# Attention, a gated FFN in FP4 and their residuals on one core: a new attention opening, presets of the residual in PSUM and another drain

## The chip, the core and the metric

One core of one Trainium2 chip. The time is the device time of one execution in microseconds. The engines are TensorE (PE in the rows, its weight loads PEld), VectorE (DVE), ScalarE (ACT), GpSimd (POOL) and SyncE (SP), which issues all DMAs here. Each runs its own instructions in order; they wait for each other by semaphores only.

## The reference, cut to what matters

x is [64, 128, 256] fp32, the context has the same shape.

```python
def attn(Q, K, V, Wq, bq, Wout, bout):          # auto-correlation attention, one head of 16 columns
    q, k, v = (Q @ Wq + bq).T, (K @ Wq + bq).T, (V @ Wq + bq).T
    corr = real(ifft(fft(q) * conj(fft(k)))).mean(axis=(0, 1))      # 128 lags
    W, I = top_k(corr, 12); W = softmax(W)
    R = sum(w * roll(v, -shift) for w, shift in zip(W, I))
    return reshape(broadcast(R, 16 heads), [B, L, 256]) @ Wout + bout
def fp4_linear(x, w):                            # both sides quantised in blocks of 16 to the E2M1 grid
    return quant(x) @ quant(w).T
x = x + attn(layernorm(x), ctx, ctx, ...)
n = layernorm(x)
x = x + fp4_linear(silu(fp4_linear(n, w_gate)) * fp4_linear(n, w_up), w_down)      # 256 -> 704 -> 256
```

## The kernel before, in words

A tile is one of the 64 sequences, 128 rows by 256 columns; two tiles make a pair, so there are NP = 32 pairs. All of x stays in SBUF (`xs`).

First phase (to about 70 us): x and the context are loaded, turned by TensorE, projected and correlated; beside it the weights are quantised. Then comes the opening of the second phase: the correlation's sum (L855), the twelve largest lags on VectorE (L1091 to L1109), two DMAs that turn the weights of the lags into the circulant matrix `cT` (L359, L361), `wp` (L867 and L1116), and the attention's output for all 64 tiles in four blocks (L875), 512 rows of 257 columns (the last is the mean that the layer norm needs). `a_sb` keeps them with `bout` added (L1119), DMAs bring them to DRAM and back to each pair's rows. The first four tiles don't wait for that: four matmuls with a 0/1 matrix `pick` (L882) spread rows of `a_sb` over PSUM, and VectorE adds them to x (L1125). Beside it TensorE turns the quantised weights (L829, L844) and ScalarE brings them to SBUF (L297, L306). `ones` matmuls (L862, L914), whose result nobody reads, fill TensorE's waits.

Second phase, stages st = -4 to 35, a software pipeline over pairs, its order written out by hand on every engine. In stage st TensorE does the gate and up matmuls of pair st (`gate_and_up`, L889 to L891, 18 a tile, of 512 and 384 columns) and the down matmuls of tiles 2st-7 and 2st-6 (`down`, 17 of 256 columns, L899 and L901); ScalarE `silu` of pair st (L621), `split_h` of pair st-1 (L562, L563, L565: 1408 columns each), `split_x` and the layer norm of later pairs; VectorE the product gate x up of pair st-1 (`gate_up`, L1145), the blocks' maxima (L1247), scales and grid (`scaling_h` L1241 writes y_h, which `split_h` reads; `offset_h` L945 and `grid_h` L1199 read what `split_h` wrote in the stage before), and the same for x; POOL the low halves of the scales and products. SP turns the products by DMA transposes (`turn_h` L383 to hqT, `turn_x` L388).

The residual of the FFN: TensorE adds x to the down product as a last fp32 matmul with the scaled identity `ident_out` (L903) for even tiles, and ScalarE scales the result to SBUF (`residual`, L626); for odd tiles up to stage 31 (`added(i)`) VectorE does scale and add in one instruction (L1214). Down products alternate between PSUM banks 6 and 7, so tile j waits for the residual of tile j-2 (`out_ready`). In the last stage pair 31 is worked on tile by tile (`last_scale`, `last_y`, `last_split`, `last_grid`), turned by DMA like the others, and the last eight tiles' residuals are ScalarE's.

Of the kernel before, what the change touches and what calls it, by code (L numbers as in the profile page):

```python
# [15 lines left out]
P = 128  # L16
# [50 lines left out]
A_BANK = (4, 6, 0, 1)  # L67
PICK_BANK = (2, 3, 5, 7)
N_PIECES = 4

# [12 lines left out]
def build(nc, x, ctx, wq, bq, wout, bout, w_gate, w_up, w_down, out):  # L83
    es = ExitStack()
    with es:
# [91 lines left out]
        pick = w_raw[:, 0:4 * P].rearrange("p (j l) -> p j l", j=4)  # L177
# [9 lines left out]
        d_prod = ctx16[:, 4 * FF:8 * FF].bitcast(F32)  # L187
        hqT = sb("hqT", [P, 4, DCH, P], F16)
# [9 lines left out]
        def bank16(k):  # L198
# [7 lines left out]
            "q_bias", "g_done", "g_col", "g_ev", "g_io", "t_steps", "t_pe", "t_exp", "t_io", "a_io0", "a_io1", "a_io2", "a_io3", "m_sums", "pick_set", "picked",  # L206
            "x1_done", "sq_done", "pool_st", "xn_ready", "x_max", "sc_steps", "sh_done", "sl", "x_split", "yx_done", "x4_steps",
            "h_steps", "h_split", "yh_done", "h4_steps", "loh", "z_lo", "z_scale", "z_sh", "z_sl", "z_y", "z_split", "z_grid", "z_done", "o_done", "o_add", "id_out",
# [105 lines left out]
        def _(sp):  # L314
# [43 lines left out]
            sp.wait_ge(s["t_steps"], 7)  # L358
# [45 lines left out]
            for st in range(FIRST, END):  # L404
# [20 lines left out]
        def _(pool):  # L425
# [923 lines left out]
```

## Time and profile before

| | |
|---|---|
| median of 3 runs | 478.52 us (478.27 to 481.03) |
| the profiled execution | 479.78 us, span 477.3 us |
| TensorE matmul busy | 445.2 us (93% of the span), 3362 |
| VectorE busy | 436.4 us (91%) |
| ScalarE busy | 384.4 us (81%) |
| GpSimd busy | 248.5 us (52%) |
| granted TensorE clock, mean | 0.982 |
| chain that ended last, by engine | PE 80%, DVE 9%, ACT 3%, DMA 3% |

Times in the rows are from the start of the span. A timeline row has start, duration, engine, line, operation and operands, and in brackets how long the engine idled before it and what released it. Records of one engine overlap a little: the next begins some 0.08 us before the one before it ends. A 128x512 or 128x256 matmul's record contains its pipeline tail, so the pace is read from start to start.

### The profile page before, as it was taken

To read this page: it belongs to the slowest core of one execution; us is meant where nothing else is said; L and a number is where in the kernel's file an instruction comes from. 1 tells how busy PE (TensorE), PEld (TensorE's weight loads), DVE (VectorE), ACT (ScalarE), POOL (GpSimd) and SP (SyncE) were. 2 spreads that over 40 slices of the span, in tenths; PEclk is the share of its full clock that TensorE was granted. 3 is DMA by queue.
4 is the path that set the end of the run, shared out by engine and by line. 5 is a ranking of instruction groups with operands and counts; after the bars stand their busy time and mean duration, and the time that the engine had idled before them with its cause. 6 is when DMAs were issued, how large, how long until landed. Compare 5 with 4: busy or idle time off the path is not lost.

```text
span 477.3 us, 9868 instructions
## 1 busy us (share of the span) xinstructions
PE 445.2 (93%) x3362; PEld 300.8 (63%) x3362; DVE 436.4 (91%) x768; ACT 384.4 (81%) x642; POOL 248.5 (52%) x338
## 2 busy tenths in 40 slices
PE   4599995978699999999999999999999999999987
PEld 4488885844366666666666666666666666666675
DVE  3699987579999999999999999999999999999982
ACT  3369969599988888888888888888888888867572
POOL 4157750544466655665555666666666655433310
PEclk9799997999999999999999999999999999999999
DMA  7999901442256678656567666676666666555565
GB/s 242 339 349 347 345 13 33 90 90 67 59 116 138 139 121 159 128 126 129 129 130 139 140 134 139 132 134 131 139 139 137 140 116 141 107 105 106 119 139 129
DMA packets 164849, 68.66 MB, mean 144 GB/s; under 512 B 129216, under 2 KB 164544, under 8 KB 164800
## 3 DMA queue, kind: packets, MB, share of 16 engines
q1 hardware_dynamic: 164800, 68.03, 62.2%
q8 instruction: 27, 0.44, 0.4%
q14 instruction: 22, 0.18, 0.1%
HBM read 27.38 MB, written 9.18 MB: 77 GB/s over the span
## 4 chain that ended last, share of the span: by engine, by line
PE 80%; DVE 9%; ACT 3%; DMA 3%; issue 2%; SPq 1%; POOL 1%; DVEq 0%; POOLq 0%; ACTq 0%
PE ps L889 16%; PE ps L890 15%; PE ps L891 15%; PE ps L899 15%; PE ps L901 8%; PE ps L903 3%; PE ps L740 2%; PE ps L750 2%; DMA ctx_sb<-in_ctx_dram 2%; PE ps L763 2%; DVE a_bst L994 1%; ACT h_c L565 1%; DMA hqT<-ctx_sb 1%; ACT h_c L562 1%; DVE hb L1145 1%
## 5 line engine op out<-in xcount | busy, mean ns | idle before, releaser
L889 PE MATMUL ps<-guT_hi,a_xT 128*128 128x512 f16 (+1 forms) x384 | 139.5, 363 | 7.9 <-DVE hb L1145 5.4
L890 PE MATMUL ps<-guT_lo,a_xT 128*128 128x512 f16 (+1 forms) x384 | 139.5, 363 | 0.0
L891 PE MATMUL ps<-guT_hi,a_xT 128*128 128x512 f16 (+1 forms) x384 | 139.4, 363 | 0.0
L899 PE MATMUL ps<-dT_hi,hqT 128*128 128x256 f16 x704 | 129.2, 273 | 2.6 <-DMA hqT<-ctx_sb 2.6
L901 PE MATMUL ps<-dT_lo,hqT 128*128 128x256 f16 x384 | 87.3, 273 | 0.0
L492 POOL TENSOR_TENSOR ctx_sb<-w_q_lo,sl 128x704 f16<-128x704 f16 x58 | 87.2, 1524 | 0.0
L621 ACT ACTIVATE w_raw<-ps,inv_gu 128x704 f32<-128x704 f32 x64 | 53.9, 841 | 33.4 <-PE ps L891 33.3
L899 PEld LDWEIGHTS ps<-dT_hi,hqT 128*128 128x128 f16 x704 | 68.9, 98 | 13.7 <-DMA hqT<-ctx_sb 3.7
L508 POOL TENSOR_TENSOR sl<-bm,sh 128x240 f16<-128x240 f32 (+2 forms) x34 | 20.5, 604 | 95.0 <-DVE y_h L1241 72.8
L889 PEld LDWEIGHTS ps<-guT_hi,a_xT 128*128 128x128 f16 x384 | 37.7, 98 | 45.8 <-DMA a_xT<-ctx_sb 8.6
L562 ACT ACTIVATE h_c<-y_h 128x1408 bf16<-128x1408 bf16 (+3 forms) x39 | 47.9, 1227 | 20.1 <-DVE y_h L1241 16.6
L891 PEld LDWEIGHTS ps<-guT_hi,a_xT 128*128 128x128 f16 x384 | 37.7, 98 | 38.9 <-issue 0.7
L890 PEld LDWEIGHTS ps<-guT_lo,a_xT 128*128 128x128 f16 x384 | 37.7, 98 | 37.0 <-issue 0.6
L1145 DVE SCALAR_TENSOR_TENSOR hb<-ps,h_in,w_raw 128x704 f32<-128x704 f32 x64 | 57.7, 939 | 0.8 <-ACT w_raw L621 0.6
L548 POOL TENSOR_TENSOR xs<-xs,w_raw 128x512 f32<-128x512 f32 x30 | 35.4, 1180 | 44.0 <-DVE x_c L949 44.0
L1247 DVE TENSOR_REDUCE bm<-hb 128x88 f32<-128x1408 f32 x31 | 50.2, 1620 | 1.1
L565 ACT ACTIVATE h_c<-h_c,root 128x1408 bf16<-128x1408 bf16 (+3 forms) x39 | 50.9, 1305 | 0.0
L1241 DVE TENSOR_TENSOR y_h<-hb,bm 128x1408 f32<-128x1408 f32 x31 | 50.0, 1614 | 0.0
L563 ACT ACTIVATE h_t<-y_h 128x1408 f16<-128x1408 bf16 (+3 forms) x39 | 47.3, 1212 | 0.0
L901 PEld LDWEIGHTS ps<-dT_lo,hqT 128*128 128x128 f16 x384 | 37.6, 98 | 9.2
L532 POOL TENSOR_TENSOR s_r<-s_ve,neg_half 128x2 f32<-128x2 f32 x32 | 36.3, 1136 | 2.7
L647 ACT ACTIVATE w_q_hi<-xs,s_nmr,s_r 128x256 f32<-128x256 f32 x64 | 34.9, 595 | 1.5 <-POOL s_nmr L534 1.5
(164 smaller groups left out, 794.9 us busy)
## 6 DMA issues: line engine op xcount, KB each, us to landing
xs<-in_x_dram SPq DMA_DIRECT2D x16, 512.0 KB, 8.4
ctx_sb<-in_ctx_dram SPq DMA_DIRECT2D x16, 512.0 KB, 7.9
out_dram<-a_xT SPq DMA_DIRECT2D x64, 128.0 KB, 2.2
w_raw<-a_scratch SPq DMA_DIRECT2D x60, 128.5 KB, 2.7
hqT<-ctx_sb SPq DMA_TRANSPOSE x64, 3.8
w_raw<-in_L_ffn_w_down_dram SPq DMA_DIRECT2D x1, 704.0 KB, 8.3
w_raw<-in_L_ffn_w_gate_dram SPq DMA_DIRECT2D x1, 640.0 KB, 5.0
w_raw<-in_L_ffn_w_up_dram SPq DMA_DIRECT2D x1, 640.0 KB, 6.3
```

The source lines that it names most:

```text
L492: pool.tensor_tensor(hq[:, j % 2, t, FF:2 * FF].rearrange("p (ih r) -> p ih r", ih=IH), h_g.bitcast(F16).rearrange("p (ih t r) -> p t ih r ...
L562: act.activation(c.bitcast(BF16), top, ACT.Square, scale=ANCHOR_SLOPE * unit).then_inc(done, 1)
L565: act.activation(c.bitcast(BF16), c.bitcast(BF16), ACT.Square, bias=root[:, 0:1]).then_inc(done, 1)
L621: act.activation(sil[:, i % 2, :], gu_out(i)[:, 0:FF], ACT.Silu, scale=inv_gu[:, 0:1]).then_inc(s["sil_done"], 1)
L889: pe.matmul(dst, xt[:, c, :], guT[0][:, c, n0:n1], start=(c == 0), stop=False)
L890: pe.matmul(dst, xt[:, c, :], guT[1][:, c, n0:n1], start=False, stop=False)
L891: last = pe.matmul(dst, xt[:, KC + c, :], guT[0][:, c, n0:n1], start=False, stop=(c == KC - 1))
L899: last = pe.matmul(dst, hqT[:, j % 4, c, :], dT_hi[:, c, :], start=(c == 0), stop=(added(j) and c == DCH - 1))
L901: pe.matmul(dst, hqT[:, j % 4, c, :], dT_lo[:, c, :], start=False, stop=False)
L1145: dve.scalar_tensor_tensor(out=h_v, in0=gu_out(i)[:, FF:2 * FF].rearrange(split, ih=IH), scalar=h_in[:, 0:1], in1=sil[:, i % 2, :].rearran ...
L1241: dve.tensor_tensor(y_h[:, :].rearrange(runs, ih=IH, il=2), hb[:, :].rearrange(runs, ih=IH, il=2), bm[:, 2, 0:RUN_H].unsqueeze(1).unsqueez ...
L1247: dve.tensor_reduce(bm[:, 0, 0:RUN_H], hb[:, :].rearrange("p (ih b il) -> p b ih il", ih=IH, il=2), AX.XY, ALU.max, apply_absolute_value=T ...
```

## The change

1. The first four tiles' attention is computed directly: POOL spreads the first rows of v over the 128 rows of each tile (`v_head`), TensorE multiplies them with `wp` into four PSUM banks (`attend_head`, 2 matmuls a tile), POOL has added `bout` to x ahead of it, VectorE adds (`add_head`). The `pick` matrix and its four matmuls go. The order on TensorE is heads 0 and 1, block 0, heads 2 and 3, blocks 1 to 3. Each of the later weight turns has another bank, the 8 filler matmuls before `cT` go, those before the first gate matmul are 20 for 28; the load of the Silu table moves ahead of the evacuations. VectorE takes the twelve largest lags straight from PSUM without the scaling.
2. Steady stages: only every fourth tile (i % 4 == 1) keeps VectorE's residual. For the other tiles 2 to 55 an fp16 matmul opens the PSUM bank (`open_down`, L1020, its product is overwritten), ScalarE writes x times `out_fac` into it (`preset_x`), the down matmuls add to it and ScalarE scales it out.
3. The last tiles: for tiles 56 to 61 the fp32 residual matmul comes first. `split_h` of pair 30 moves ahead of the last `silu`, with residual(56) ahead of both, and `last_split(0)` ahead of residual(57). Pair 30's products are made tile by tile. Pair 31 is turned by TensorE (`turn_last`, 22 transposes), four parts copied to SBUF by ScalarE and one by VectorE, and its residuals are VectorE's (`last_residual`).
4. Small moves: `w_inverses` of the down weights after the last q/k evacuation, `largest_x(3)` between two `gate_up`, the evacuations of the down weights later.

```diff
         def added(i):
-            return i % 2 == 1 and i // 2 < NP - 4
+            return i % 4 == 1 and i // 2 < NP - 4
+
+        def preset(i):
+            return i >= 2 and i % 4 != 1 and i // 2 < NP - 4
+
+        def n_added(i):
+            return (min(i, 2 * (NP - 4) - 1) + 3) // 4
+
+        def n_preset(i):
+            return i + 1 - 1 - n_added(i)
         def out_ready(eng, i):
             if added(i):
-                eng.wait_ge(s["o_add"], i // 2 + 1)
+                eng.wait_ge(s["o_add"], n_added(i))
             elif i >= 0:
-                eng.wait_ge(s["o_done"], i // 2 + 1 if i < 2 * (NP - 4) else i + 1 - (NP - 4))
+                eng.wait_ge(s["o_done"], i + 1 - n_added(i))
+
...
             act.wait_ge(s["t_steps"], 3)
-            act.activation(wexp[:, :], corr[:, 0, 0:P], ACT.Exp, bias=nmx[:, 0:1]).then_inc(s["t_exp"], 1)
-            evacuate_weights(act, range(GU_FILLS))
+            act.activation(wexp[:, :], bank(4)[:, 0:P], ACT.Exp, bias=nmx[:, 0:1], scale=1.0 / (B * DH)).then_inc(s["t_exp"], 1)
+            act.preload_act_table(ACT.Silu)
+            evacuate_weights(act, range(EARLY))
             w_hi(N_GU)
+            evacuate_weights(act, range(EARLY, EARLY + 1))
             w_hi(N_GU + 1)
-            act.preload_act_table(ACT.Silu)
+            evacuate_weights(act, range(EARLY + 1, GU_FILLS))
...
+            def preset_x(i):
+                if preset(i):
+                    act.wait_ge(s["o_open"], n_preset(i))
...
+                    evacuate_weights(act, range(GU_FILLS + 1, GU_FILLS + 2))
                 elif st < NP:
                     residuals(2 * st - 8)
                     square_x(st + 4)
                     scale_high(st)
+                    residuals(2 * st - 7)
                     silu(2 * st)
+                    preset_x(2 * st - 6)
+                    if st == 1:
+                        evacuate_weights(act, range(GU_FILLS + 2, GU_FILLS + 3))
+                    if st == 2:
+                        evacuate_weights(act, range(GU_FILLS + 4, len(FILLS)))
+                    normalise_x(st + 3)
+                    if st == NP - 1:
+                        residual(2 * NP - 8)
+                        split_h(j)
+                    silu(2 * st + 1)
+                    preset_x(2 * st - 5)
+                    if st < NP - 1:
+                        split_h(j)
+                    split_x(n)
                     if st == 1:
                         evacuate_weights(act, range(GU_FILLS + 3, GU_FILLS + 4))
-                    normalise_x(st + 3)
-                    residuals(2 * st - 7)
-                    silu(2 * st + 1)
-                    split_h(j)
-                    split_x(n)
-                    if st == 1:
-                        evacuate_weights(act, range(GU_FILLS + 4, len(FILLS)))
                 elif st == NP:
-                    residual(2 * st - 8)
-                    residual(2 * st - 7)
                     last_split(0)
-                    residual(2 * st - 6)
-                    residual(2 * st - 5)
+                    residual(2 * NP - 7)
+                    residual(2 * NP - 6)
+                    residual(2 * NP - 5)
                     last_split(1)
-                elif st > NP + 1:
-                    residuals(2 * st - 8)
-                    residuals(2 * st - 7)
+                    keep_turned(0)
+                    keep_turned(1)
+                    residual(2 * NP - 4)
+                    keep_turned(2)
+                    keep_turned(4)
+                    residual(2 * NP - 3)
...
-            pe.wait_ge(s["v_ev"], 2)
-            for _ in range(8):
-                pe.matmul(bank(6)[:, 0:P], ones[:, :], ident[:, :], start=True, stop=True)
...
-            for g in range(4):
+
+            def attend_head(j):
                 for h in range(2):
-                    if g == 0:
-                        pe.wait_ge(s["t_steps"], 10 + h)
+                    if j == 0:
+                        pe.wait_ge(s["t_steps"], 9 + h)
+                    last = pe.matmul(bank(HEAD_BANK[j])[:, 0:DA], v_head[:, h, j, :], wp[:, h, :], start=(h == 0), stop=(h == 1))
+                last.then_inc(s["direct"], 1)
...
+
+            pe.wait_ge(s["spread_v"], 1)
+            pe.wait_ge(s["w_ev"], EARLY)
+            attend_head(0)
+            attend_head(1)
+            attend(0)
+            attend_head(2)
+            attend_head(3)
+            for g in range(1, 4):
+                attend(g)
...
             def down(j):
-                dst = bank(6 + j % 2)[:, 0:D]
-                pe.wait_ge(hT[j % 4], 16 * (j // 4 + 1))
-                out_ready(pe, j - 2)
+                final = j // 2 == NP - 1
+                late = j >= 2 * (NP - 4) and not final
+                dst = bank(2 * (1 - j % 2) if final else 6 + j % 2)[:, 0:D]
+                if final:
+                    if j % 2 == 0:
+                        turn_last(0)
+                elif preset(j):
+                    pe.wait_ge(s["o_set"], n_preset(j))
+                else:
+                    out_ready(pe, j - 2)
+                if late:
+                    pe.matmul(dst, ident_out[:, :], xs[:, j, :], start=True, stop=False)
+                if not final:
+                    pe.wait_ge(hT[j % 4], 16 * (j // 4 + 1))
                 for c in range(DCH):
-                    last = pe.matmul(dst, hqT[:, j % 4, c, :], dT_hi[:, c, :], start=(c == 0), stop=(added(j) and c == DCH - 1))
+                    if final and j % 2 == 0 and c in (0, CUT):
...
+                    last = pe.matmul(dst, hqT[:, j % 4, c, :], dT_hi[:, c, :], start=(c == 0 and not late and not preset(j)),
+                                     stop=(c == DCH - 1 and (j > 0)))
                     if c < LOCH:
                         pe.matmul(dst, hqT[:, j % 4, c, :], dT_lo[:, c, :], start=False, stop=False)
-                if not added(j):
+                if j == 0:
                     last = pe.matmul(dst, ident_out[:, :], xs[:, j, :], start=False, stop=True)
                 last.then_inc(s["d_done"], 1)
...
+            def turn_last(t):
+                for k in range(len(TURNS)):
+                    if TURNS[k][0] == t:
+                        dst = turned(k)[0]
+                        c0, c1 = PARTS[TURNS[k][1]]
+                        pe.wait_ge(s["z_done"], 2 * t + (1 if c0 == 0 else 2))
+                        for c in range(c0, c1):
+                            last = pe.transpose(dst[:, c - c0, :], hq[:, (NP - 1) % 2, t, c * P:(c + 1) * P], ident16[:, :])
+                        last.then_inc(s["z_turn"], 1)
...
-            for _ in range(28):
+            for _ in range(20):
                 pe.matmul(bank(4)[:, 0:P], ones[:, :], ident[:, :], start=True, stop=True)
...
+            def open_down(j):
+                if preset(j):
+                    out_ready(pe, j - 2)
+                    pe.matmul(bank(6 + j % 2)[:, 0:D], ident16[:, :], dT_hi[:, 0, :], start=True, stop=False).then_inc(s["o_open"], 1)
...
+                    if n >= 4:
+                        open_down(2 * n - 6)
+                        open_down(2 * n - 5)
                     gate_and_up(2 * n + 1)
...
+            add_head(0)
+            keep_attn(0)
+            add_head(1)
+            for g in range(1, 4):
+                keep_attn(g)
...
-                    high_h(p)
-                    low_h(p)
+                    for t in range(2):
+                        turned_products(p, t)
                     gate_up(2 * j + 1)
                     last_scale(1)
                     last_y(1)
                     last_grid(0)
                     last_grid(1)
+                    dve.wait_ge(s["z_turn"], 4)
+                    dve.wait_ge(s["d_done"], 2 * NP - 4)
+                    src, dst = turned(3)
+                    dve.tensor_copy(dst, src).then_inc(s["z_ev_v"], 1)
+                    last_residual(0)
+                    last_residual(1)
 _INS = ['x', 'ctx_1024', 'L0_xattn_Wq', 'L0_xattn_bq', 'L0_xattn_Wout', 'L0_xattn_bout', 'L0_ffn_w_gate',
```

On TensorE, in a steady even stage, between the gate matmuls of its two tiles. Before, the second tile's follow at once:

```order
L890 MATMUL ps<-guT_lo,a_xT 128x384
L891 MATMUL ps<-guT_hi,a_xT 128x384
L889 MATMUL ps<-guT_hi,a_xT 128x512 [waits h_steps,xT0]
L890 MATMUL ps<-guT_lo,a_xT 128x512
L891 MATMUL ps<-guT_hi,a_xT 128x512
```

And now (L953 to L955 are the same three lines; `o_add` counts VectorE's residuals, `o_done` ScalarE's):

```order
L954 MATMUL ps<-guT_lo,a_xT 128x384
L955 MATMUL ps<-guT_hi,a_xT 128x384
L1020 MATMUL ps<-dT_hi,ident 128x256 [waits o_done]
L1020 MATMUL ps<-dT_hi,ident 128x256 [waits o_add]
L953 MATMUL ps<-guT_hi,a_xT 128x512 [waits h_steps,xT0]
L954 MATMUL ps<-guT_lo,a_xT 128x512
```

Two openings stand between them, the second of which waits for the residual that VectorE does in the same stage. In odd stages there is one, with a wait for `o_done`.

On ScalarE, stages 31 and 32, before (the row with x2 is both `silu` of pair 31):

```order
L626 ACTIVATE a_xT<-ps,inv_out 128x256 [waits stored2,d_done]
L668 ACTIVATE sh<-bm 128x176 [waits h4_steps,x4_steps,sl,sc_steps]
L621 ACTIVATE w_raw<-ps,inv_gu 128x704 [waits gate_done] x2
L562 ACTIVATE h_c<-y_h 128x1408 [waits h4_steps,yh_done]
L563 ACTIVATE h_t<-y_h 128x1408
L565 ACTIVATE h_c<-h_c,root 128x1408 [waits h_split]
L626 ACTIVATE a_xT<-ps,inv_out 128x256 [waits stored0,d_done]
L626 ACTIVATE a_xT<-ps,inv_out 128x256 [waits stored1,d_done]
L632 ACTIVATE sh<-bm 128x88 [waits h4_steps,z_scale]
L637 ACTIVATE w_q_lo<-w_raw 128x8x88 [waits z_y]
```

And now (L656 is `residual`, L651 `silu`, L590 to L593 `split_h`, L662 to L670 `last_split`):

```order
L656 ACTIVATE a_xT<-ps,inv_out 128x256 [waits stored3,d_done]
L651 ACTIVATE w_raw<-ps,inv_gu 128x704 [waits gate_done]
L656 ACTIVATE a_xT<-ps,inv_out 128x256 [waits stored0,d_done]
L590 ACTIVATE h_c<-y_h 128x1408 [waits h4_steps,yh_done]
L591 ACTIVATE h_t<-y_h 128x1408
L593 ACTIVATE h_c<-h_c,root 128x1408 [waits h_split]
L651 ACTIVATE w_raw<-ps,inv_gu 128x704 [waits gate_done]
L662 ACTIVATE sh<-bm 128x88 [waits h4_steps,z_scale]
L667 ACTIVATE w_q_lo<-w_raw 128x8x88 [waits z_y]
L668 ACTIVATE w_q_lo<-w_raw 128x8x88
L670 ACTIVATE w_q_lo<-w_q_lo,root 128x8x88 [waits z_split]
L656 ACTIVATE a_xT<-ps,inv_out 128x256 [waits stored1,d_done]
```

The third row is residual(56), which waits for down(56); `split_h` and the last `silu` stand behind it.

## Rows read from the trace of the kernel before

**Rows 1.** The chain of waits, by time: start us, duration, engine, tile, line.
```profile
141.14 0.55 PE ps L899 x5
...
445.62 0.55 PE ps L899 x5
```

**Rows 2.** The timeline of VectorE, three stages' marks.
```profile
142.15 0.88 DVE L945 TENSOR_TENSOR h_t<-h_c,h_t 128x1408 f16<-128x1408 bf16 x1
...
300.39 0.88 DVE L945 TENSOR_TENSOR h_t<-h_c,h_t 128x1408 f16<-128x1408 bf16 x1
...
303.66 0.48 DVE L1214 SCALAR_TENSOR_TENSOR a_xT<-ps,inv_out,xs 128x256 f32<-128x256 f32 x1
304.05 0.89 DVE L1266 RECIPROCAL bm<-bm 128x120 f32<-128x120 f32 x1
...
311.69 0.88 DVE L945 TENSOR_TENSOR h_t<-h_c,h_t 128x1408 f16<-128x1408 bf16 x1
```

**Rows 3.** The timeline of TensorE in the same stage.
```profile
302.94 0.38 PE L889 MATMUL ps<-guT_hi,a_xT 128*128 128x512 f16 x1
...
308.37 0.60 PE L903 MATMUL ps<-xs,ident_out 128*128 128x256 f32 x2
308.80 0.27 PE L899 MATMUL ps<-dT_hi,hqT 128*128 128x256 f16 x1
308.91 0.27 PE L901 MATMUL ps<-dT_lo,hqT 128*128 128x256 f16 x1
```

**Rows 4.** The timeline of ScalarE in the same stage.
```profile
301.51 0.46 ACT L626 ACTIVATE a_xT<-ps,inv_out 128x256 f32<-128x256 f32 x1
301.87 0.50 ACT L657 ACTIVATE w_raw<-xs,s_nm 128x256 f32<-128x256 f32 x1
...
305.74 0.85 ACT L621 ACTIVATE w_raw<-ps,inv_gu 128x704 f32<-128x704 f32 x1 [0.77 <-PE ps L891]
307.24 1.38 ACT L562 ACTIVATE h_c<-y_h 128x1408 bf16<-128x1408 bf16 x1 [0.66 <-DVE y_h L1241]
...
309.79 1.46 ACT L565 ACTIVATE h_c<-h_c,root 128x1408 bf16<-128x1408 bf16 x1
```

**Rows 5.** The drain: timelines of ScalarE and TensorE, then the chain.
```profile
453.11 1.37 ACT L562 ACTIVATE h_c<-y_h 128x1408 bf16<-128x1408 bf16 x1
...
474.64 0.48 ACT L626 ACTIVATE a_xT<-ps,inv_out 128x256 f32<-128x256 f32 x1 [1.81 <-PE ps L903]
...
455.43 0.27 PE L899 MATMUL ps<-dT_hi,hqT 128*128 128x256 f16 x1
...
466.30 3.50 DMA hqT<-ctx_sb
```

**Rows 6.** The opening: timelines of TensorE and VectorE, then stretches, granted clock after POOL.
```profile
74.78 0.46 PE L855 MATMUL ps<-dg,ones 128*128 128x128 f32 x2 [2.54 <-issue]
...
82.94 1.03 PE L867 MATMUL ps<-wout_sb,cT 128*128 128x257 f32 x4
84.21 1.98 PE L875 MATMUL ps<-wp,v_all 128*128 128x257 f32 x8 [0.24 <-DVE wp L1116]
...
100.32 0.39 PE L889 MATMUL ps<-guT_hi,a_xT 128*128 128x512 f16 x1 [2.54 <-DMA a_xT<-ctx_sb]
...
89.70 0.43 DVE L1119 TENSOR_TENSOR a_sb<-ps,bout_bc 128x257 f32<-128x257 f32 x1 [0.44 <-PE ps L875]
...
91.50 0.69 DVE L1271 TENSOR_REDUCE bm<-w_q_hi 128x32 f32<-128x512 f32 x1 [0.72 <-ACT w_q_hi L647]
...
76.00:82.00 6.00, 4.33 (x32) 4.08 (x33) 5.45 (x15) 6.00 (x11) 0.00 (x0) 0.50 0.12 33
82.00:100.00 18.00, 15.03 (x112) 13.29 (x110) 9.90 (x25) 12.15 (x28) 9.15 (x15) 1.00 0.42 89
```

**Rows 7.** The issue of cT, by its line.
```profile
L361 SPq DMA_DIRECT2D cT<-w_scratch x1: 333/333/333, 79.6 to 79.6; - x1
...
DMA to landing us min/median/max: 1.8/1.8/1.8
```

More of the change, by code:

```diff
@@ L693, in _ @@
                     square_x(st + 4)
-                    if st >= -2:
-                        evacuate_weights(act, range(GU_FILLS + 2 + st, GU_FILLS + 3 + st))
+                    if st == -2:
+                        evacuate_weights(act, range(GU_FILLS, GU_FILLS + 1))
                 elif st == 0:
@@ L702, in _ @@
                     split_x(n)
-                    evacuate_weights(act, range(GU_FILLS + 2, GU_FILLS + 3))
+                    evacuate_weights(act, range(GU_FILLS + 1, GU_FILLS + 2))
                 elif st < NP:
@@ L877, in _ @@
                 last.then_inc(s["t_pe"], 1)
-                if g == 1:
-                    pe.wait_ge(s["t_steps"], 12)
-                    pe.wait_ge(s["pick_set"], 2)
-                    for j in range(4):
-                        pe.matmul(bank(PICK_BANK[j])[:, 0:DA], pick[:, j, :], a_sb[:, 0, :], start=True, stop=True).then_inc(s["picked"], 1)
+            pe.wait_ge(s["spread_v"], 1)
[7 more added lines that the diff above has]
+                attend(g)
             def gu_bank(i, k):
@@ L907, in _ @@
+            pe.wait_ge(s["t_steps"], 14)
             pe.wait_ge(s["w_ev"], GU_FILLS)
@@ L1209, in low_h, with turned_products, last_residual @@
                 times_runs(hq[:, p % 2, :, FF:2 * FF], h_g, sl[:, (p + 1) % 2, 0:2 * RUN_H], RUN_H).then_inc(s["z_lo"], 1)
+            def turned_products(p, t):
+                dve.wait_ge(h4, K_HQ * p + 2)
+                need(dve, hT[2 * (p % 2) + t], 16 * (p // 2))
+                dve.wait_ge(s["sl"], p + 2 - SC0)
+                for part, scale in ((0, sh), (1, sl)):
+                    last = dve.tensor_tensor(
+                        hq[:, p % 2, t, part * FF:(part + 1) * FF].rearrange("p (ih r) -> p ih r", ih=IH), tile_of(h_g.bitcast(F16), t),
+                        scale[:, (p + 1) % 2, t * RUN_H:(t + 1) * RUN_H].unsqueeze(1).broadcast_to([P, IH, RUN_H]), ALU.mult)
+                last.then_inc(s["z_lo"], 1)
+            def last_residual(t):
+                i = 2 * NP - 2 + t
+                dve.wait_ge(s["d_done"], i + 1)
+                dve.wait_ge(stored[i % 4], 16 * (i // 4))
+                dve.scalar_tensor_tensor(out=of[:, i % 4, :], in0=bank(2 * (1 - t))[:, 0:D], scalar=inv_out[:, 0:1], in1=xs[:, i, :],
+                                         op0=ALU.mult, op1=ALU.add).then_inc(s["o_last"], 1)
             def residual(i):
@@ L1283, in _ @@
                     gate_up(2 * j)
+                    if st == 1:
+                        largest_x(3)
                     gate_up(2 * j + 1)
@@ L1297, in _ @@
                         grid_x(xa)
-                    if pair_ok(st - 4):
+                    if tile_ok(2 * st - 7) and added(2 * st - 7):
                         residual(2 * st - 7)
```

168 lines of the change are left out of this document (105 added, 63 removed).

## The prediction

> **What bounds the kernel now.** I read the chain of waits first, then the timelines of one period on VectorE, TensorE and ScalarE, then the drain and the opening. The chain gives the period: in stages 3 to 30 the same place of the down matmuls comes back at 141.14 and 445.62 us, 27 periods of 11.277 us [rows 1], TensorE all the way. VectorE is as full: its `offset_h` starts at 142.15 and 300.39, 14 periods of 11.303 us, and at 311.69 again, each instruction issued before its predecessor's record ends [rows 2]. So two engines set the pace together, TensorE a little ahead. ScalarE has holes: 0.77 us before the second `silu` (it waits for TensorE) and 0.66 us before `split_h` (it waits for y_h) [rows 4]. Whatever is taken from one of the two full engines pays only if the other gets shorter too, and if no new wait ties them. I take even stages st to be those in which VectorE keeps its residual.
>
> **Steady stages, the work.** TensorE: the fp32 residual matmul takes 308.80 - 308.37 = 0.43 us, a 256-column fp16 matmul 0.11 [rows 3]. Per two stages two of the first go (-0.86) and three openings come (+0.33): 22.55 - 0.53 = 22.02 us. VectorE: every second residual goes, with its slot of 304.05 - 303.66 = 0.39 us [rows 2]: two stages of 22.60 become 22.21. ScalarE gets three presets and a residual per two stages. No row shows ScalarE writing a 128x256 tile to PSUM; the residual that reads PSUM takes a slot of 301.87 - 301.51 = 0.36 us [rows 4], the Square from SBUF a record of 0.50. I take 0.36, ends 0.30 and 0.50. That is 1.44 us per two stages against 2 x 1.43 us of holes: it fits. The skill's page ScalarE: Activation LUTs (What ACT_TABLE_LOAD costs) gives 186 ns plus 0.833 ns an element, 93 ns for a pointer scale and 93 ns of overlap, an estimate of 0.40 us; by it the sum would grow by 0.04 us per two stages.
>
> **Steady stages, the new wait.** `open_down(2n-5)` stands between the two tiles' gate matmuls, and in even stages it waits for the residual of tile 2n-7, which VectorE runs at 303.66 to 304.14, 3.75 us after its `offset_h` [rows 2]. TensorE starts the second tile's gates at 302.94 now [rows 3]. So it stops there. Behind it in the queue are those gates; behind them `silu(2st+1)`, and behind that on ScalarE, which runs in order, the preset and `split_h`, for which VectorE's next `offset_h` waits. Followed through: residual done 304.14, opening at 304.18, gates from 304.29 (+0.11), `silu` 2.80 us after the gates' start as now (305.74 - 302.94) at 307.09, preset 0.75 us later at 307.84, `split_h` at 308.20 instead of 307.24, its three instructions 4.01 us (307.24 to 309.79 + 1.46), `offset_h` at 312.25 instead of 311.69 [rows 2 to 4]. An even stage takes 11.86 us from one `offset_h` to the next. The odd one has no such wait (its opening waits for a residual that ScalarE does first) and VectorE's work of 11.30 - 0.39 = 10.91. Together 22.77 against TensorE's 22.55 now, +0.22. From stage 4 to 30 there are 13 such pairs: +2.9 us. The first stop, in stage 4, shifts TensorE once: 1.35 us by the rows at 303, less the 0.35 by which VectorE had not yet fallen behind TensorE then (14 periods of 0.026): +1.0. After stage 30 one fp32 matmul less stands before down(56): -0.4. Sum **+3.4 us**, bounds: all of it hidden, below; links 0.3 us longer, +7.
>
> **Drain.** TensorE's down(56) ends at 455.43, 21.9 us before the end of the span [rows 5]. Now `split_h(30)` starts at 453.11, right after the last `silu`; its record shows no wait for y_h, so that was there before. In the new order ScalarE does residual(56) before it, and that waits for down(56), which TensorE issues after all gates: `split_h(30)` starts at D + 0.45, with D the end of down(56), instead of D - 2.3: 2.8 us later. VectorE's products (four of 704 columns for two of 1408) take the same. `last_split(0)` now precedes residual(57), so that ends near D + 7.9 (split 4.0, silu 0.75, last_split 2.4, residual 0.5 behind D + 0.4), and on SP store(57) stands ahead of the transposes of tiles 60 and 61: these are issued at D + 8.5 and land at D + 12.1 by the 3.50 us of the last pair's [rows 5]. down(60) and down(61), 17 matmuls of 0.11 each and one 0.43 between, end at D + 16.3; TensorE turns tile 62 (11 transposes, 0.65), ScalarE copies 640 columns (0.65 + 0.15), then 1.1 + 0.6 + 0.75 for down(62) in two pieces around tile 63's turning, 1.85 for down(63): D + 22.0. VectorE's residual is 0.5 with its wait, the store 2.2 as now (477.3 less 474.64 + 0.48): D + 24.6 against D + 21.9: **+2.7 us**. The turning itself saves: 3.50 us of DMA become about 1.5. No row shows a PSUM copy of fp16 columns here; I took 0.65 from `evacuate_weights`, whose four copies in 2.87 us appear in the opening; ends 0.4 and 0.9. Bounds of the drain: +1 and +4.
>
> **Opening.** Gone are VectorE's scaling of the correlation (0.3), four pick matmuls and the wait on them; new are four direct pairs. cT is issued at 79.6 and lands 1.8 us later, so at 81.4, 81.1 with the 0.3 [rows 7]; now TensorE comes to it at 82.94, after filler matmuls [rows 6]. Four 128x257 fp32 matmuls (eight records) take 1.98 us with the last one's tail, some 0.46 each. The old row has 12 of them behind wp, the new one 16, +1.8 us, and VectorE must keep the last of the four blocks before `largest_x(0)`, which starts at 91.50 now, while the last block is kept at 89.70 [rows 6]. The first pair's x1 comes earlier, but this in-order queue gives most back. The granted clock is 0.50 from 76 to 82, which is 1.2 GHz, and full from 82 on [rows 6]; without the fillers the first three or four matmuls run at 1.2 GHz, twice as long: `largest_x(0)` at about 91.1 if it rises near 83, 92.0 if near 85.5, 90.4 if no matmul is slow. I take **-0.3 us**, ends -1.1 and +0.5. ScalarE's table load moves from a hole into the way of the evacuations, 1.28 us by the profile; those matmuls wait for cT anyway. The same section of the skill's ScalarE page puts a switch of set at about 2.66 us with its drain; by it the second half of the evacuations is 1.4 us later and the opening comes to about +0.3 instead of -0.3. No row shows the drain, since the engine idled behind the load. The other edits (`w_inverses`, the place of `largest_x(3)`, of out_fac, the moved evacuations) lie beside waits for ScalarE or POOL and count 0.
>
> **Sum.** +3.4 + 2.7 - 0.3 = +5.8 us. The profiled run took 479.78 us (span 477.3 and 2.5 around it), 1.3 us over the median of 478.52. I put the sum on the median: **484.3 us**, 1.2% slower.
>
> **Rivals.** (a) The loop is hidden: if the links behind the opening are 0.56 us shorter than I added (11.86 against 11.30), `offset_h` isn't late, and VectorE's work decides, 22.21 for two stages, 13 x -0.34 = -4.4, +1.0 - 0.4 at the edges, drain and opening as above: -1.4, so 477.1. For it: ScalarE's holes. Against: the 0.66 us hole lies behind the preset, not before it. (b) The drain alone is as its name says: TensorE's down(57) to (61) run through and only the turning remains, D + 20.2, so 3.4 - 1.7 - 0.3 = +1.4: 479.9. It would need `split_h(30)` not to stand behind residual(56), that is, down(56) done before 453.11; TensorE's row at 455.43 speaks against it [rows 5]. (c) Both: -4.4 + 0.6 - 1.7 - 0.3 = -5.8, 472.7: faster than before. It decides from the point where TensorE's stop costs ScalarE less than its two holes. (d) As forecast, and the clock falls before the first gate matmuls: 20 fillers instead of 28 leave TensorE idle for about 3.0 us; in the profile it fell after 2.54 us of idling and one short matmul at 74.78, and held through 2.54 us of idling before 100.32 [rows 6]. The second tile's gates would end about 2 us later: 486.3. The skill's page TensorE: Matmul & The Clock Gate (HAM oscillation) says that a stream with a long enough wait between bursts restarts at half clock.
>
> **Numbers.** As forecast 0.50, (a) 0.15, (b) 0.16, (c) 0.08, (d) 0.11. One per cent, 4.8 us, is about what can be told here from no change: over 483.3 is slower, under 473.7 faster. Of the forecast's 0.50, with bounds 481 to 488, 0.37 lies over 483.3, and all of (d): 0.48. Of (c) 0.06 and of (a) 0.02 lie under 473.7: 0.08. The rest, 0.44, is same. The range reaches from 476.0, leaving out (c) and part of (a), to 487.5; the forecast alone has 481 to 487.5.
>
> **What would show it.** Steady: in every second stage TensorE idle about 0.8 us before the opening, released by VectorE's residual; VectorE idle 0.5 us before `offset_h`, released by ScalarE; a period of 22.8 for two stages. If it is 22.2 with no idle on VectorE, (a) holds. Drain: ScalarE idle for some 4 us before residual(56), the transposes of tile 60 behind store(57), and 24 to 25 us from the end of down(56) to the end. Opening: `largest_x(0)` within 1 us of 91.5, the granted clock at 1.00 from the first gate matmul. Presets of over 0.7 us, or a drain under 22 us, would make the sum wrong.

## The result, and the profile after

The changed kernel takes **493.5 us** (median of 4 runs, 490.3 to 494.5) against 478.5 before: ratio 1.029, interval 1.023 to 1.035. The forecast was 484.3 with a range of 476.0 to 487.5: the sign was right, the size was not, and the time lies outside the range. The profiled run took 494.3 us, its span is 492.6 against 477.3. The 15.3 us of difference, by marks that both traces have (the first `offset_h` over 1408 columns; the start of the first matmul behind down(56), which is the D of the prediction):

| stretch | before | after | difference | forecast |
|---|---|---|---|---|
| start to first `offset_h` | 119.55 | 123.68 | +4.1 | -0.3 |
| first `offset_h` to D | 335.88 | 343.78 | +7.9 | +3.4 |
| D to the end | 21.87 | 25.14 | +3.3 | +2.7 |

The page of the changed kernel shows the clock first. In the chain of waits TensorE had 80% before; now it shares with VectorE, as two engines do that stop each other. Busy time of each engine, TensorE's granted clock in 40 slices of 12.3 us, and the chain by engine:

```profile
PE 447.0 (91%) x3343; PEld 297.7 (60%) x3343; DVE 440.2 (89%) x758; ACT 405.2 (82%) x699; POOL 246.6 (50%) x340
...
PEclk9899995979889999999999999999999999999989
...
PE 34%; DVE 31%; issue 18%; ACT 10%; DMA 3%; SPq 1%; DVEq 1%; POOL 0%; ACTq 0%; POOLq 0%
```

**The loop.** The waits of the changed kernel between 150 and 430 us (us in total, times, longest):

```profile
PEld ps L1020 <- DVE a_xT L1346: 15.8, 13, 1.3
PE ps L1020 <- DVE a_xT L1346: 11.7, 12, 1.0
...
DVE h_t L1048 <- ACT h_c L593: 6.0, 12, 0.5
...
POOL xs L576 <- DVE x_c L1052: 47.7, 23, 2.6
```

That is the forecast wait: TensorE stops 1.0 us in every even stage (forecast about 0.8), and the `offset_h` that ends it is 0.5 us late. Now VectorE's timeline of one even stage (with its residual, L1346) and one odd stage (without), start and duration in us, and beneath it GpSimd's addition of the attention rows:

```profile
285.76 0.88 DVE L1048 TENSOR_TENSOR h_t<-h_c,h_t 128x1408 f16<-128x1408 bf16 x1
...
289.03 0.48 DVE L1346 SCALAR_TENSOR_TENSOR a_xT<-ps,inv_out,xs 128x256 f32<-128x256 f32 x1
289.42 0.89 DVE L1398 RECIPROCAL bm<-bm 128x120 f32<-128x120 f32 x1
290.23 0.47 DVE L1265 TENSOR_TENSOR ctx_sb<-x_c,sh 128x512 f16<-128x512 f16 x1
...
297.64 0.89 DVE L1048 TENSOR_TENSOR h_t<-h_c,h_t 128x1408 f16<-128x1408 bf16 x1 [0.50 <-ACT h_c L593]
...
300.92 0.90 DVE L1398 RECIPROCAL bm<-bm 128x120 f32<-128x120 f32 x1
301.73 0.87 DVE L1265 TENSOR_TENSOR ctx_sb<-x_c,sh 128x512 f16<-128x512 f16 x1
...
308.96 0.88 DVE L1048 TENSOR_TENSOR h_t<-h_c,h_t 128x1408 f16<-128x1408 bf16 x1
```
```profile
289.25 1.17 POOL L576 TENSOR_TENSOR xs<-xs,w_raw 128x512 f32<-128x512 f32 x1 [1.55 <-DVE x_c L1052]
...
301.14 1.18 POOL L576 TENSOR_TENSOR xs<-xs,w_raw 128x512 f32<-128x512 f32 x1 [2.55 <-DVE x_c L1052]
```

The even stage takes 297.64 - 285.76 = 11.88 us (forecast 11.86). The odd one takes 11.32, not 10.91: `offset_h` comes at 308.96, and VectorE has no idle time in between. The residual is gone (0.39) and the product of x that follows the reciprocal has become 0.40 longer. It ends 0.28 us after GpSimd's addition does (302.32 + 0.28 = 301.73 + 0.87), as in the even stage (290.42 + 0.28 = 290.23 + 0.47). The product's wait is not idle time at a semaphore: it lies inside the record of the instruction, and the first section's "by semaphores only" is not the whole of it. In the kernel before the same pair was there to be seen, in the first stages, which have no residual yet, and at the end, where GpSimd adds nothing (VectorE's timeline of the kernel before, and GpSimd's):

```profile
122.81 0.90 DVE L1266 RECIPROCAL bm<-bm 128x120 f32<-128x120 f32 x1
123.62 0.87 DVE L1150 TENSOR_TENSOR ctx_sb<-x_c,sh 128x512 f16<-128x512 f16 x1
...
304.86 0.47 DVE L1150 TENSOR_TENSOR ctx_sb<-x_c,sh 128x512 f16<-128x512 f16 x1
...
406.59 0.36 DVE L1150 TENSOR_TENSOR ctx_sb<-x_c,sh 128x512 f16<-128x512 f16 x1
```
```profile
123.03 1.18 POOL L548 TENSOR_TENSOR xs<-xs,w_raw 128x512 f32<-128x512 f32 x1 [5.26 <-DVE x_c L949]
```

**The opening.** Stretches of the changed kernel (width, then busy us and instructions of each engine from PE to POOL, then TensorE's granted clock, DMA share, GB/s):

```profile
76.00:82.00 6.00, 4.03 (x22) 2.85 (x22) 5.79 (x10) 5.99 (x9) 1.54 (x2) 0.50 0.11 33
82.00:91.50 9.50, 9.12 (x32) 7.50 (x32) 3.58 (x10) 4.66 (x12) 2.58 (x4) 0.74 0.04 14
...
100.00:111.00 11.00, 9.24 (x32) 3.86 (x33) 6.28 (x11) 6.74 (x18) 5.11 (x10) 0.69 0.43 93
```

The clock was 1.00 from 82 on before [rows 6]. Now it is at half, 1.2 GHz, through the first attention matmuls (to 87.0), and falls again at 100.7, before the first gate matmuls, where TensorE waits 3.44 us instead of 2.54 (TensorE's timeline):

```profile
93.63 4.68 PE L1009 MATMUL ps<-ident,ones 128*128 128x128 f32 x40
101.75 0.61 PE L953 MATMUL ps<-guT_hi,a_xT 128*128 128x512 f16 x1 [3.44 <-DMA a_xT<-ctx_sb]
102.15 0.63 PE L954 MATMUL ps<-guT_lo,a_xT 128*128 128x512 f16 x1
```

The clock is not all of the 4.1 us. GpSimd's addition stops VectorE here too, as in the odd stages (VectorE, then GpSimd, in the changed kernel):

```profile
96.21 0.86 DVE L1048 TENSOR_TENSOR x_t<-x_c,x_t 128x512 f16<-128x512 bf16 x1 [1.83 <-ACT x_c L593]
...
99.71 1.56 DVE L1366 TENSOR_TENSOR w_raw<-w_q_hi,bm 128x512 f32<-128x512 f32 x1
```
```profile
95.60 1.18 POOL L576 TENSOR_TENSOR xs<-xs,w_raw 128x512 f32<-128x512 f32 x1 [2.43 <-DMA w_raw<-a_scratch]
...
99.54 1.18 POOL L576 TENSOR_TENSOR xs<-xs,w_raw 128x512 f32<-128x512 f32 x1
```

Before, these two took 0.43 and 0.69. `largest_x(0)` starts 0.86 us later than before, from there to the third `largest_x` (104.69, before 102.43) VectorE loses another 1.40 us, 1.30 of it in these two rows, and from there to the second `gate_up` it takes 7.31 us for 5.45, at half clock: 4.1 together.

**The drain.** ScalarE, then VectorE, then SP's queue in the changed kernel:

```profile
467.66 0.47 ACT L656 ACTIVATE a_xT<-ps,inv_out 128x256 f32<-128x256 f32 x1 [5.98 <-PE ps L983]
468.04 1.37 ACT L590 ACTIVATE h_c<-y_h 128x1408 bf16<-128x1408 bf16 x1
...
474.96 0.82 ACT L656 ACTIVATE a_xT<-ps,inv_out 128x256 f32<-128x256 f32 x2
```
```profile
472.06 0.89 DVE L1048 TENSOR_TENSOR h_t<-h_c,h_t 128x1408 f16<-128x1408 bf16 x1 [4.19 <-ACT h_c L593]
```
```profile
475.87 3.03 SPq L402 DMA_TRANSPOSE hqT<-ctx_sb  x2
```

`split_h(30)` starts behind residual(56) at D + 0.6 (forecast D + 0.45, before D - 2.3 [rows 5]) and the transposes of tile 60 are issued at D + 8.4 (forecast D + 8.5): as forecast. ScalarE's wait before residual(56) is longer than the forecast "some 4 us", and TensorE stands for 3.26 us before down(59), until residual(57) is done.

### The profile page after: what moved, and what is told of

Same layout as the page of the kernel before. It is cut to its first block, busy times and chain, and to the rows that moved or that the text cites. A ratio compares the mean times of both kernels' runs of the same rounds, so it can differ in the third digit from the quotient of the medians.

```text
span 492.6 us, 9874 instructions
## 1 busy us (share of the span) xinstructions
PE 447.0 (91%) x3343; PEld 297.7 (60%) x3343; DVE 440.2 (89%) x758; ACT 405.2 (82%) x699; POOL 246.6 (50%) x340
## 4 chain that ended last, share of the span: by engine, by line
PE 34%; DVE 31%; issue 18%; ACT 10%; DMA 3%; SPq 1%; DVEq 1%; POOL 0%; ACTq 0%; POOLq 0%
PE ps L953 6%; PE ps L955 6%; PE ps L954 6%; DVE hb L1260 5%; ACT h_c L593 4%; DVE y_h L1373 4%; PE ps L983 4%; ACT h_c L590 4%; DVE ctx_sb L1265 3%; DVE bm L1379 3%; DVE w_q_lo L1314 2%; DVE x_t L1048 2%; DVE x_c L1052 2%; PE ps L814 2%; DVE bm L1403 2%
## 5 line engine op out<-in xcount | busy, mean ns | idle before, releaser
L953 PE MATMUL ps<-guT_hi,a_xT 128*128 128x512 f16 (+1 forms) x384 | 141.1, 367 | 8.7 <-DVE hb L1260 5.3
L954 PE MATMUL ps<-guT_lo,a_xT 128*128 128x512 f16 (+1 forms) x384 | 141.0, 367 | 0.0
L955 PE MATMUL ps<-guT_hi,a_xT 128*128 128x512 f16 (+1 forms) x384 | 140.8, 367 | 0.0
L983 PE MATMUL ps<-dT_hi,hqT 128*128 128x256 f16 x704 | 126.3, 275 | 0.5 <-ACT hqT L676 0.5
L986 PE MATMUL ps<-dT_lo,hqT 128*128 128x256 f16 x384 | 88.5, 275 | 0.0
L651 ACT ACTIVATE w_raw<-ps,inv_gu 128x704 f32<-128x704 f32 x64 | 53.9, 842 | 34.8 <-PE ps L955 34.2
L953 PEld LDWEIGHTS ps<-guT_hi,a_xT 128*128 128x128 f16 x384 | 38.0, 99 | 46.6 <-DMA a_xT<-ctx_sb 9.4
L955 PEld LDWEIGHTS ps<-guT_hi,a_xT 128*128 128x128 f16 x384 | 38.1, 99 | 40.0 <-issue 2.6
L590 ACT ACTIVATE h_c<-y_h 128x1408 bf16<-128x1408 bf16 (+3 forms) x39 | 47.6, 1220 | 6.8 <-DVE y_h L1066 4.1
L593 ACT ACTIVATE h_c<-h_c,root 128x1408 bf16<-128x1408 bf16 (+3 forms) x39 | 50.9, 1304 | 0.0
L1048 DVE TENSOR_TENSOR h_t<-h_c,h_t 128x1408 f16<-128x1408 bf16 (+3 forms) x39 | 30.9, 793 | 12.7 <-ACT h_c L593 12.7
```

The lines of the kernel that those rows point to most:

```text
L590: act.activation(c.bitcast(BF16), top, ACT.Square, scale=ANCHOR_SLOPE * unit).then_inc(done, 1)
L593: act.activation(c.bitcast(BF16), c.bitcast(BF16), ACT.Square, bias=root[:, 0:1]).then_inc(done, 1)
L651: act.activation(sil[:, i % 2, :], gu_out(i)[:, 0:FF], ACT.Silu, scale=inv_gu[:, 0:1]).then_inc(s["sil_done"], 1)
L953: pe.matmul(dst, xt[:, c, :], guT[0][:, c, n0:n1], start=(c == 0), stop=False)
L954: pe.matmul(dst, xt[:, c, :], guT[1][:, c, n0:n1], start=False, stop=False)
L955: last = pe.matmul(dst, xt[:, KC + c, :], guT[0][:, c, n0:n1], start=False, stop=(c == KC - 1))
```

## The experiments

Ten kernels were run, each against the kernel before on the same chip; its median there was 480.1, 479.5 and 479.9 us in the three batches. The edits are to the changed kernel. A period is the time from one `offset_h` to the next.

**e1_no_presets**
```diff
 def added(i):
-    return i % 4 == 1 and i // 2 < NP - 4
+    return i % 2 == 1 and i // 2 < NP - 4
 def preset(i):
-    return i >= 2 and i % 4 != 1 and i // 2 < NP - 4
+    return False
...
-                if j == 0:
+                if not (late or final or added(j)):
                     last = pe.matmul(dst, ident_out[:, :], xs[:, j, :], start=False, stop=True)
```


> The changed kernel with its steady part taken back: VectorE keeps every second residual, no tile is preset, the fp32 residual matmul stands at the end again; the new opening and the new drain stay. In the changed kernel's trace the first offset_h is 4.1 us late, from there to the end of down(56) it loses 8.1 us, and from there to the end 3.1. If these three are separate, this run takes 478.5 + 4.1 + 3.1 = 485.7 us, its offset_h come every 11.30 us and no offset_h waits for ScalarE before the last ones. If the lost time of the loop comes from the late opening (another phase between the engines) and not from the presets, the period stays above 11.4 and it takes over 490.

Measured 483.7 us, ratio 1.010 (1.007 to 1.013). Periods of 11.30 as before, first to 28th `offset_h` 304.93 us (before 304.94, changed kernel 312.63), D to the end 25.06. So the loop's loss is that of part 2 of the change, and the drain's does not depend on it. Under 485.7 because the first `offset_h` came at 120.0: the same opening, but here the clock rose at about 82 us, as before, and not at 87, it was at half for 3.4 us around the first gates and not for 6.8, and VectorE's second multiply of x took 0.69, not 1.56.

**e2_open_late**
```diff
                         open_down(2 * n - 6)
-                        open_down(2 * n - 5)
                     gate_and_up(2 * n + 1)
+                    if n >= 4:
+                        open_down(2 * n - 5)
```


> One line moved: TensorE's open_down(2n-5), which waits for VectorE's residual, stands behind the second tile's gate matmuls, no longer ahead of them. If the stop of TensorE there (1.0 us in every even stage) is what makes offset_h 0.5 us late, the even stages fall from 11.88 to 11.31 us, the odd ones stay at 11.32, and the time falls by 13 x 0.57 = 7.4, to 486.1. If it is ScalarE's added work (three presets and a residual in two stages) that makes offset_h late, the idle time before offset_h stays at 0.5 us, and the time at 493.

Measured 483.1 us, 1.007 (1.004 to 1.010). From the fifth period on even and odd stages take 11.30 us (the third still takes 12.13), the wait of `offset_h` for ScalarE is gone, and first to 28th `offset_h` is 305.68 us: 7.0 less, near the 7.4 expected. Of the 9.5 us between the two profiled spans 2.1 more are the opening (first `offset_h` at 121.6, other gaps of clock). ScalarE has room for three presets and a residual; the place of one opening matmul was the fault. But the odd stages hold the loop at the old pace, though TensorE has 0.5 us less to do in two stages:

```profile
285.45 0.47 DVE L1266 TENSOR_TENSOR ctx_sb<-x_c,sh 128x512 f16<-128x512 f16 x1
...
296.36 0.86 DVE L1266 TENSOR_TENSOR ctx_sb<-x_c,sh 128x512 f16<-128x512 f16 x1
```

**e3_open_late_add_late**: e2 and
```diff
                     if st >= 1:
-                        pool.wait_ge(s["x4_steps"], K_XQ * (st + 1) + 2)
+                        pool.wait_ge(s["x4_steps"], K_XQ * (st + 2))
```


> As e2_open_late, and GpSimd adds the attention rows to x (128x512 fp32, 1.18 us) only when VectorE is done with both products of x, not when their first one starts. In the changed kernel the first of these products takes 0.87 us in stages without a VectorE residual and 0.47 in those with one, and 0.36 in the last stages, where GpSimd adds nothing. If the overlap with GpSimd's addition makes it long, all take 0.36, the odd stages need 10.81 us of VectorE and TensorE's 22.02 us per two stages decides: 13 x 1.15 = 15 us less than the changed kernel, 478.5. If the length has another cause (its position behind the reciprocal), it stays at 0.87 and the time is that of e2_open_late, 486.

Measured 499.3 us, 1.042 (1.040 to 1.044): neither of the two expected times. The first product takes 0.36 us in even and odd stages, so its length came from GpSimd. But the addition now falls beside the two multiplies with both inputs in SBUF; it takes 2.44 us instead of 1.18, since it waits for the first, and the second waits for it (VectorE, then GpSimd):

```profile
306.01 0.36 DVE L1266 TENSOR_TENSOR ctx_sb<-x_c,sh 128x512 f16<-128x512 f16 x1
306.29 0.41 DVE L1266 TENSOR_TENSOR ctx_sb<-x_c,sl 128x512 f16<-128x512 f16 x1
306.62 1.62 DVE L1374 TENSOR_TENSOR y_h<-hb,bm 128x1408 f32<-128x1408 f32 x1
308.15 1.67 DVE L1367 TENSOR_TENSOR w_raw<-w_q_hi,bm 128x512 f32<-128x512 f32 x1
```
```profile
306.84 2.44 POOL L576 TENSOR_TENSOR xs<-xs,w_raw 128x512 f32<-128x512 f32 x1 [2.97 <-DVE ctx_sb L1266]
309.24 0.64 POOL L577 TENSOR_TENSOR s_nm<-neg_mean,w_raw 128x2 f32<-128x2 f32 x1
```

That second multiply takes 0.68 us elsewhere. The periods are 12.17 and 11.78: e2's 11.30 with 0.99 more for it and 0.11 or 0.50 less for the product. The Trainium skill's page SBUF — State Buffer (SBUF: two separate sides) says that VectorE with two SBUF inputs and a GpSimd operation that reads SBUF exclude each other for the whole instruction, and that the one that starts first keeps the other out. The trace agrees, in both directions: GpSimd waited 1.26 us and VectorE 0.99.

One more row of this run bears on the opening: TensorE waits as long before the first gates as in the changed kernel, behind the same fillers, and here the clock stays at 1.00 (TensorE's timeline, then the stretch).

```profile
101.96 0.39 PE L953 MATMUL ps<-guT_hi,a_xT 128*128 128x512 f16 x1 [3.43 <-DMA a_xT<-ctx_sb]
```
```profile
100.00:111.00 11.00, 9.04 (x50) 4.62 (x51) 7.17 (x12) 8.21 (x20) 5.80 (x10) 1.00 0.43 96
```

**e4_fillers**
```diff
             for f in range(EARLY, GU_FILLS):
                 transpose_weights(f)
+                if f == EARLY:
+                    pe.wait_ge(s["v_ev"], 2)
+                    for _ in range(6):
+                        pe.matmul(bank(5)[:, 0:P], ones[:, :], ident[:, :], start=True, stop=True)
...
-            for _ in range(20):
+            for _ in range(30):
```


> Only the opening's filler matmuls: six are put between the weight transposes where TensorE idled for 2.7 us, and 30 instead of 20 stand before the first gate matmuls. If the granted clock of 0.50 (73 to 87 us and again 101 to 107 us) costs the opening its 4.1 us, it is at 1.00 from about 84 us and stays there, the first offset_h comes at 120.5 instead of 123.7, and the time falls by about 3 us, to 490.5. If the new order of the attention matmuls and the late transfers cost it, the clock rises but the first offset_h stays near 123, and the time within 1 us of 493.5.

Measured 490.2 us, 1.022 (1.020 to 1.025). First `offset_h` at 118.8, 4.9 us earlier than in the changed kernel's profile and 0.7 earlier than before; clock and work of the stretches:

```profile
82.00:91.50 9.50, 7.98 (x46) 6.77 (x46) 5.25 (x13) 5.33 (x14) 3.84 (x7) 1.00 0.17 35
...
100.00:111.00 11.00, 11.00 (x66) 5.74 (x64) 8.78 (x16) 9.85 (x26) 5.51 (x12) 1.00 0.33 73
```

`largest_x(0)` came at 90.57: with the clock up, the new opening is 0.9 us faster than the old one up to there. Not all of the 4.9 us is the clock's: here VectorE's second multiply of x began 0.04 us before GpSimd's addition and took 0.69, and the addition waited (VectorE, then GpSimd).

```profile
97.59 0.69 DVE L1370 TENSOR_TENSOR w_raw<-w_q_hi,bm 128x512 f32<-128x512 f32 x1
```
```profile
97.63 1.68 POOL L576 TENSOR_TENSOR xs<-xs,w_raw 128x512 f32<-128x512 f32 x1
```

**e9_fill30_only**: of e4 the second edit alone.

> The changed kernel with 30 instead of 20 fillers before the first gate matmuls, nothing else. In the changed kernel TensorE idles for 3.44 us there and the first 14 gate matmuls run at half clock; with the wait cut to about 1 us the clock should stay at 1.00 and the time from the first gate matmul to the second gate_up should fall from 10.25 us to 7.5 (as in e4 and the kernel before), 493.5 - 2.5 = 491. If the fall before the attention matmuls (73 to 87 us) is what costs, the time stays at 493.5.

Measured 491.0 us, 1.025 (1.022 to 1.028). The wait before the first gate matmul is 1.02 us, the clock there 1.00, and from that matmul to the second `gate_up` it takes 8.45 us, not 7.5. The missing 1.0 us is GpSimd's addition, which began 0.04 us before VectorE's second multiply of x (VectorE, then GpSimd):

```profile
98.54 1.68 DVE L1366 TENSOR_TENSOR w_raw<-w_q_hi,bm 128x512 f32<-128x512 f32 x1
```
```profile
98.50 1.18 POOL L576 TENSOR_TENSOR xs<-xs,w_raw 128x512 f32<-128x512 f32 x1
```

The other 10.25 - 8.45 = 1.8 us are the second fall. From the third `largest_x` to the second `gate_up`, which leaves that stop out, it is 5.44 us here, 5.43 in e3 and 7.31 in the changed kernel: 1.9.

**f1_open_late_no_add**: e2 and
```diff
-                    pool.tensor_tensor(x1, x1, attn[:, n % 2, :, 0:D], ALU.add)
```


> As e2_open_late, and GpSimd's addition of the attention rows (128x512 fp32) is left out, so that the sum of x and attention is missing in tiles 4 to 63. In e3 the addition moved behind the products and stopped VectorE's next multiply instead (0.68 to 1.67 us). If the two engines' exclusion is the whole loss in the loop, the products take 0.36 us everywhere, VectorE needs 11.19 and 10.80 us in the even and odd stages, TensorE 22.02 in both, and the two-stage period is 22.0 to 22.1 instead of 22.60: about 12 x 0.55 = 6.6 us under e2_open_late, 476.5. If something else holds the odd stages at 11.3, the period stays at 22.6 and the time at 483.

Measured 476.1 us, 0.991 (0.988 to 0.994), by a kernel that leaves out the sum of x and attention for tiles 4 to 63. Periods 11.21 and 10.80, together 22.01, as TensorE's 22.02, and VectorE is as full. This is about what the loop would give if the two engines did not exclude each other.

**e5_split_first**
```diff
-                        residual(2 * NP - 8)
                         split_h(j)
+                        residual(2 * NP - 8)
```


> The changed kernel with split_h(30) ahead of residual(56) on ScalarE, nothing else. If the drain alone gains, 25.0 us become about 20 and the time is 488.5; if not, within 1 us of 493.5.

Measured 487.8 us, 1.017 (1.015 to 1.020). D at 467.28, end at 488.1: 20.8 us instead of 25.1. TensorE no longer waits for residual(57), only for a transpose (0.73) and for ScalarE's copy (0.46); ScalarE:

```profile
462.70 1.38 ACT L590 ACTIVATE h_c<-y_h 128x1408 bf16<-128x1408 bf16 x1 [1.20 <-DVE y_h L1373]
...
467.48 0.47 ACT L656 ACTIVATE a_xT<-ps,inv_out 128x256 f32<-128x256 f32 x1 [0.77 <-PE ps L983]
```

**f3_no_presets_fillers_split_first**: e1, e4 and e5 together.

> As e1_no_presets (new opening, new drain, steady stages as before), with the fillers of e4 and split_h(30) ahead of residual(56). If the three stages add up: the first offset_h at about 119 (119.55 before), the loop as before, and a drain of 20 us instead of 21.9: 478.5 - 0.7 - 2 = 475.8 us, a little faster than before. If the drain isn't shortened by the order on ScalarE, it takes 480 to 481.

Measured 478.5 us, 0.997 (0.996 to 0.999): 0.3% faster, less than expected. The drain is 20.8 us, but the first `offset_h` came at 120.7, 1.9 us after e4's. The clock was at half again from 81 to 84.5 us although the six fillers took 2.7 us, about as in e4 (2.9), and `largest_x(0)` came 0.8 us after e4's. VectorE's second multiply took 1.66 us, since GpSimd's addition began just ahead of it: the other 1.0. So e4's early fillers don't hold the clock up in every kernel.

**f2_open_late_fillers_split_first**: e2, e4 and e5 together.

> The changed kernel with all three repairs: the opening matmul behind the second tile's gates (e2), the fillers (e4), and in stage 31 ScalarE does split_h(30) before residual(56), which waits for down(56). If split_h(30) behind that residual is what lengthens the drain, it starts at 461.7 of the changed kernel's time and not at 468.0, TensorE's stop of 3.3 us after down(58) is gone, and the drain is about 20 us from the end of down(56), not 25.0: 493.5 - 9.3 (e2 and its late opening) - 3 - 5 = about 477. If the drain is bound by its chain of last_split and turned tiles, it stays over 24 and the time is 481 or more.

Measured 476.8 us, 0.994 (0.992 to 0.996): all parts of the change kept, and 0.6% faster than before. First `offset_h` 120.4, first to 28th 305.4, drain 20.8.

**g6_f2_more_fillers**: f2 with 12 instead of 6 of the early fillers.

> As f2 (all three repairs), with 12 instead of 6 fillers between the weight transposes. In f2 the six ran at full clock, took 1.4 us, TensorE idled for 2 us behind them and the clock was 0.50 again for the attention matmuls (80 to 86.7 us): largest_x(0) at 92.13. Where it was at 1.00 from 82 on, largest_x(0) came at 90.4 to 90.6. If the twelve keep the clock up, the time falls by up to 1.7 us, to 475; if they run at half clock (0.47 us each), the transposes start up to 1.8 us later and nothing is gained.

Measured 476.4 us, 0.993 (0.991 to 0.995), the fastest, but its interval overlaps f2's. The clock stayed up until about 82.9 us and was at half from there to 86.3; `largest_x(0)` at 92.01. With six more fillers the fall came later (82.9 us for 79.7 in f2) and did not go; the 1.7 us were not there to be had this way.

## Why the prediction was wrong, step by step

- **Bound and the new wait in even stages: right.** 11.86 forecast, 11.88 measured; e2 takes it away by one line. Rivals (a) and (c), the wait hidden, did not happen.
- **"VectorE: every second residual goes, with its slot of 0.39" and "the odd one has ... 10.91": wrong, the step that failed in the loop.** The odd stage is 11.32. The residual reads PSUM and stood in front of the product while GpSimd's addition ran: it was cover. Without it the product waits 0.40 us more. Eleven odd stages with 11.32 instead of 10.91 are 4.5 us, which is what the loop was missed by (7.9 against 3.4). That the products were of unequal length, 0.87, 0.47 and 0.36, stood in the trace of before; I subtracted a slot instead of asking what ran beside it. f1 shows the price: 22.60 - 22.01 = 0.59 us in two stages.
- **Opening, "I take -0.3": wrong, by 4.4 us in the profiled run.** The structure was judged well (-0.9 to `largest_x(0)` with the clock up, in e4; "92.0 if it rises near 85.5", 92.36 measured with a rise at 87.0). Three terms failed. The clock was taken to rise near 83 us, and rose at 87: `largest_x(0)` is 0.86 us later than before and not 0.3 earlier. Rival (d), with a chance of 0.11, is what happened before the gates; its price of 2.0 us was near (1.8 by e9, 1.9 by the marks). And GpSimd's additions, put at nothing, took 1.3 us from VectorE. I had set the range by one fall or the other, not both. Whether the fall at the gates follows from 20 fillers for 28 is not certain: e3 has the same fillers and the same wait, and no fall.
- **Drain, +2.7: right** (25.1 us against 24.6 forecast, and 25.06 in e1, where nothing is preset); e5 shows the cause, `split_h(30)` behind residual(56), and the 20.8 that remain without it are near rival (b)'s D + 20.2.
- **Presets at 0.36: slightly low.** Their slot is 0.40 (289.24 to 289.64), within the bounds. At 0.40 for 0.36 three presets cost 0.12 us more in two stages, not the 0.04 that the prediction adds; it changes nothing, since e2 shows room for them.

Left open: why the clock's fall and rise before the attention matmuls come at different times in kernels with the same opening (rise at 82 us in e1, near 87 in the changed kernel and e5). The work there starts up to 0.6 us apart in these profiles; no run changes that alone. By `largest_x(0)`, 92.36 against 90.40 in e1, it carries about 2 us of the changed kernel's time. Probably it carries much of the spread too: the mean clock was 0.975 in the run of 490.3 us and 0.962 in that of 494.5. Open too is why the clock fell before the gates in the changed kernel and not in e3, and what sets whether GpSimd's additions in the opening begin just before or just after VectorE's instruction.

## What to carry to other kernels

Before counting an instruction on VectorE as saved, look at what GpSimd does at that moment and at the durations of the next instruction in stages that lack it: a PSUM read can be the cover under which GpSimd uses SBUF. A matmul that only prepares a bank must not stand ahead of work that others wait for; it belongs where its wait is already over. Shortening filler matmuls is an edit of its own: a fall of the clock cost 1.9 us here. One profile of an opening is not enough to price it, since kernels with the same opening differed by 2 us up to `largest_x(0)`.

## What the runs showed of the hardware

- A 128x512 fp16 product on VectorE takes 0.36 us alone, and 0.87 when GpSimd's addition of the same size in fp32 is under way; a 128x512 fp32 multiply takes 0.69 alone and 1.56 to 1.68 then; that addition takes 1.18 us alone and 2.44 behind a 1.62 us multiply of VectorE. The reciprocal (0.89) and the residual that reads PSUM (0.48) ran beside it at the length that they have in f1, without the addition. Of two such instructions 0.04 us apart the later one waited, VectorE's in e9, GpSimd's in e4.
- A wait of 3.44 us on TensorE after 4.68 us of fillers was followed by a clock of 0.50 for the first 5.7 us of the next work; waits of 0.7 to 1.0 us after 6.0 to 6.9 us of fillers (e4, e9, f2, f3, g6) were not. The wait's length alone does not decide: 2.8 to 3.5 us (e1, f1, e2, e5) were followed by a fall, 3.43 (e3) and 2.54 (before) were not, and 2.3 to 2.7 us before the gates at 118 to 120 were (e9, f3, e3).
- ScalarE writes a 128x256 fp32 tile from SBUF to PSUM in a slot of 0.40 us, the next instruction starting that much later.
